# Query and key parts in a scratch buffer: which copies are stored, and which are made by the loads

## The chip, the cores and the metric

The kernel runs on one core of one Trainium2 chip. The metric is device time in microseconds (us); lower is better. Three runs of the kernel before gave 1540.12, 1537.32 and 1542.91 us; their median is 1540.12 us.

## The reference, cut to what matters

The program is three residual blocks over x of shape (8, 512, 128), eight batches of 512 tokens:

```python
x = x + 0.5 * ffn(layernorm(x))     # attention with 16 heads of 8, then a mixture of 8 experts
x = x + attn(layernorm(x))          # 16 query heads of 8, 4 key/value heads, rotary positions
x = x + 0.5 * ffn(layernorm(x))     # the first block again, same weights
# each attention: softmax(q @ k.T / sqrt(8)) @ v, then a projection
```

Each block has one attention over 512 x 512 scores for each of 16 heads and 8 batches, so there are 24 batch attentions in all. The expert part takes, for each token, the expert with the largest gate logit.

## The kernel before, in words

**Tiling.** A batch has 16 heads. Four heads make a *group* (G = 4 groups a batch, J = 4 heads in a group), so there are 24 x 4 = 96 groups. The function `stream` is built twice: with `label` 0 it handles the 8 batches (32 groups) of the first block, with `label` 1 the 16 batches (64 groups) of the second and third. The tokens' expert work is cut into blocks (`experts`), which stand between the steps of the end of one stream and of the opening of the next.

**Split of q and k.** Scores are made by TensorE in float32r. To keep precision, q and k are each split into a high part `hi` and a low part `lo` (the rest), and a score is the contraction over stacked rows: per head 8 rows of each of four products hi*hi, hi*lo, lo*hi, lo*lo. In a tile of 64 partitions, the first 32 rows (`ROWS` = 4 x 8) of `c.Q` hold q parts and those of `c.K` hold k parts. Before, Q has the parts in the order hi, hi, lo, lo and K in the order hi, lo, hi, lo. Behind them come two rows of Q in which `rows_of_max` writes the high and low parts of the row maxima, against rows of -1 in K, so that the transposed scores come out with the maximum already subtracted. The rest of Q's 64 rows of a tile is zero.

**How parts get there.** For batch b, ScalarE copies the projected q and k out of PSUM (`copy_qk`, L1084 and L1086; rotated ones by `high_part`), and `lo` is made by a subtraction: on GpSimd (`low_part`, L719) for batches 1 and later, on VectorE (`low_first`) for batch 0. `hi` and `lo` lie as [128 partitions, 512] (i = 0 is q, i = 1 is k). They go to HBM scratch, `c.q_scratch` and `c.k_scratch`, by `store` (L456), one DMA of 256 KB for each stored part. For batch 0 of a stream ScalarE's queue stores the high parts and SyncE's queue the low ones, with the semaphores `first_stored`; for all others GpSimd's queue does both, with the semaphores `stored`. Before, q_scratch has 32 rows a tile, with each part twice, so q takes four stores a batch, and k takes two.

**Loads.** For each group n, `load(n)` in the SyncE program brings both tiles (2 x 64 partitions) from scratch into one of five slots of Q and K. It first waits for the scores of the group that had the slot, then for q's stores (`stored(sp, 0, ...)`, only at n = 1 and at the first group of a batch), clears 16 rows of each tile from `zero_rows` (L571; not for n < 5 of label 0), loads Q with two DMAs of 128 KB (L582), waits for k's stores likewise, and loads K with four DMAs of 64 KB (L589): each tile twice from the same 16 rows. Group 0 of a stream doesn't go through scratch: `straight` (L466) copies its parts within SBUF.

**Order of the work.** The order on every engine is fixed when the program is built (`Plan`). In the steady stretch, step (n, kt) of TensorE makes four score tiles for the row maxima of group n + 2 (L844), four transposed score tiles of group n for the exponential (L860), and the weighting by v (L873). VectorE reduces the first kind to maxima (L1239), ScalarE exponentiates the second (L1210). The maxima of group n + 1 are split (L1247, L1249), turned by TensorE (L851), copied to SBUF (L1261), and written into Q by SyncE's queue (`rows_of_max`, L601). On that queue the order in the loop over n is: rows_of_max(n + 1), load(n + 4), then a weight load or two. In the opening of a stream's main part it is load(1), load(2), load(3), rows_of_max(0), rows_of_max(1), load(4). TensorE's main part turns the maxima of group 0, waits for the loads of group 1 (`loaded(1)`), makes the maxima scores of group 1, and begins step (0, 0), whose scores wait for the rows of rows_of_max(0).

Of the kernel before, what the change touches and what calls it, by code (L numbers as in the profile page):

```python
# [19 lines left out]
F32 = mybir.dt.float32  # L20
# [8 lines left out]
H, HD = 16, 8  # L29
QT = S // P  # L30
NT = B * QT
G, J = 4, 4
NG = B * G
# [11 lines left out]
KSLOT = PAIRS * S  # L45
TILE = 64
ROWS = 4 * HD
# [7 lines left out]
SLOTS = 5  # L55
# [20 lines left out]
def wait(eng, sem, value):  # L76

    if isinstance(value, int) and value <= 0:
        return
    eng.wait_ge(sem, value)  # L80
# [33 lines left out]
def sems(ctx, nc, tag, names):  # L114

    handles, fields, values = [], [], []
    for entry in names.split():
        name, _, n = entry.partition(":")
        new = [nc.alloc_semaphore(name=f"{tag}_{name}{i}") for i in range(int(n or 1))]
        handles += new  # L120
        fields.append(name)
        values.append(new if n else new[0])

    def clear():
        nc.clear_and_free_semaphores(handles)
        nc.all_engine_barrier()

    ctx.callback(clear)
    return namedtuple("Sems", fields)(*values)
# [259 lines left out]
def stream(nc, c, ctx, a, label, kinds, past, blocks):  # L389
# [6 lines left out]
    if True:  # L396
        s = sems(ctx, nc, f"s{label}", "filled freed evacuated first max_hi split recip max_rows:5 q_loaded:5 k_loaded:5 "
                 "scores probs pv out_copied links dve_links first_stored:2 var_ready std_ready normed renormed stats:2 moments:2 added combined roped hi lo:2 "
                 "stored:2 k_first choices onehot chosen located scattered:2 tabled table tails:2")
# [42 lines left out]

        def stored(eng, i, b):

            size = (64, 32)[i]
            if b in (1, 2):
                eng.wait_ge(s.first_stored[i], size)
            wait(eng, s.stored[i], size * (b - 1))

        def store(eng, i, b, done, parts):  # L450

            at = b % B * G
            for part in parts:
                for copy in range(2 - i):
                    r = HD * ((2 - i) * part + copy)
                    eng.dma_start((c.q_scratch, c.k_scratch)[i][at:at + G, :, r:r + HD, :].rearrange("g t d n -> (g t) (d n)"),  # L456
                                  (hi, lo)[part](b)[i]).then_inc(done, 16)
                    yield

        def straight(eng, i, part):  # L460

            dst, done = ((c.Q, s.q_loaded[0]), (c.K, s.k_loaded[0] if label else s.k_first))[i]
            for tile in range(2):
                for copy in range(2):
                    r = TILE * tile + HD * (2 * part + copy if i == 0 else 2 * copy + part)
                    eng.dma_start(dst[r:r + HD, 0:KSLOT].bitcast(F32).rearrange("d (a n) -> d a n", a=PAIRS),  # L466
                                  (hi, lo)[part](0)[i][2 * HD * tile:2 * HD * (tile + 1), :]).then_inc(done, 16)
                    yield
# [97 lines left out]
        def sync(sp):  # L566
# [6 lines left out]
            def load(n):  # L573
                if n >= SLOTS:
                    sp.wait_ge(s.scores, QT * J * (n - SLOTS + 1))
                g = n % SLOTS
                if n == 1 or n % G == 0:
                    stored(sp, 0, n // G + 1)
                if n >= SLOTS or label:
                    clear_rows(g)  # L580
                for tile in range(2):
                    sp.dma_start(c.Q[TILE * tile:TILE * tile + ROWS, g * KSLOT:(g + 1) * KSLOT].bitcast(F32),  # L582
                                 c.q_scratch[n % NG, tile, :, :]).then_inc(s.q_loaded[g], 16)
                if n == 1 or n % G == 0:
                    stored(sp, 1, n // G + 1)
                for tile in range(2):
                    for copy in range(2):
                        r = TILE * tile + 2 * HD * copy
                        sp.dma_start(c.K[r:r + 2 * HD, g * KSLOT:(g + 1) * KSLOT].bitcast(F32),  # L589
                                     c.k_scratch[n % NG, tile, :, :]).then_inc(s.k_loaded[g], 16)  # L590

            def rows_of_max(n):

# [235 lines left out]
        def tensor(pe):  # L829
# [154 lines left out]
                        project(kind, i)  # L984

            def loaded(n):
                pe.wait_ge(s.q_loaded[n % SLOTS], 32 * (1 + label) + 96 * (n % SLOTS == 0) + 64 * (n // SLOTS))
                if n % SLOTS or label:
                    pe.wait_ge(s.k_loaded[n % SLOTS], 64 * (n // SLOTS + 1) + 64 * (n % SLOTS == 0))
                else:  # L990
                    pe.wait_ge(s.k_first, 128)
                    wait(pe, s.k_loaded[0], 64 * (n // SLOTS))
# [729 lines left out]
def build(nc, a, out):  # L1722
    with ExitStack() as ctx:
# [3 lines left out]
        c = Core()  # L1727
# [36 lines left out]
        c.blocks, c.thresh, c.down = sb("blocks", [P, NBLK]), sb("thresh", [P, HT_ROWS]), sb("down", [P, E])  # L1764
        c.banks = banks = ctx.enter_context(nc.psum_tensor("banks", [P, 8 * 512], F32))
        c.bank = [banks[:, i * 512:(i + 1) * 512] for i in range(8)]
        c.q_scratch = nc.dram_tensor("q_scratch", [NG, 2, ROWS, KSLOT], F32).ap()
        c.k_scratch = nc.dram_tensor("k_scratch", [NG, 2, 2 * HD, KSLOT], F32).ap()
        c.zero_rows = nc.dram_tensor("zero_rows", [2 * HD, KSLOT], F32).ap()
        c.sorted_x = nc.dram_tensor("sorted_x", [HALVES * (E + 1) * REGION, W], F32).ap()  # L1770
# [96 lines left out]
```

## Time and profile before

| | |
|---|---|
| median of three runs | 1540.12 us |
| the profiled execution's own time | 1544.99 us |
| its span, first to last instruction | 1543.3 us |
| granted TensorE clock, mean | 0.965 |
| TensorE / VectorE / ScalarE / GpSimd busy | 90% / 76% / 71% / 42% |
| moved by DMA | 137.57 MB, mean 89 GB/s |
| read from HBM / written to HBM | 79.05 / 53.51 MB |

The profile is one execution. Its own time holds 1.7 us beside the span. Busy shares are means over stages that have different limits: from about 60 to 445 us and from about 620 to 1400 us the two streams run in their steady stretch; between and behind them stands the expert work. Two stretches matter for what the change touches: the opening of the first stream (20 to 60 us) and that of the second (580 to 615 us), in which the first loads from scratch are made.

### The profile page before, as it was taken

To read this page: it belongs to the slowest core of one execution; us is meant where nothing else is said; L and a number is where in the kernel's file an instruction comes from. 1 tells how busy PE (TensorE), PEld (TensorE's weight loads), DVE (VectorE), ACT (ScalarE), POOL (GpSimd) and SP (SyncE) were. 2 spreads that over 40 slices of the span, in tenths; PEclk is the share of its full clock that TensorE was granted. 3 is DMA by queue.
4 is the path that set the end of the run, shared out by engine and by line. 5 is a ranking of instruction groups with operands and counts; after the bars stand their busy time and mean duration, and the time that the engine had idled before them with its cause. 6 is when DMAs were issued, how large, how long until landed. Compare 5 with 4: busy or idle time off the path is not lost.

```text
span 1543.3 us, 34954 instructions
## 1 busy us (share of the span) xinstructions
PE 1388.1 (90%) x12036; PEld 678.6 (44%) x12036; DVE 1177.7 (76%) x1898; ACT 1102.0 (71%) x2124; POOL 644.8 (42%) x983
## 2 busy tenths in 40 slices
PE   3699999999999886999999999999999999999975
PEld 1233334344339874333333333333333343335875
DVE  6788888888955255888888888888888888883541
ACT  2387877787775452788888888887878877777543
POOL 5222344542226555434554353133234544223743
PEclk8699999999999987999999999999999999999998
DMA  5344433432112315423332333333333333201234
GB/s 130 96 134 121 107 102 108 113 95 83 44 29 64 105 52 150 108 67 95 99 84 74 96 95 95 94 81 82 86 92 88 83 91 102 65 23 42 75 95 119
DMA packets 101485, 137.57 MB, mean 89 GB/s; under 512 B 29792, under 2 KB 72160, under 8 KB 101312
## 3 DMA queue, kind: packets, MB, share of 16 engines
q1 hardware_dynamic: 70768, 85.69, 19.6%
q0 software_dynamic: 24256, 45.31, 12.0%
q10 hardware_dynamic: 6288, 4.34, 1.0%
q8 instruction: 100, 1.64, 0.4%
q14 instruction: 73, 0.60, 0.1%
HBM read 79.05 MB, written 53.51 MB: 86 GB/s over the span
## 4 chain that ended last, share of the span: by engine, by line
PE 55%; DVE 27%; issue 7%; DMA 5%; POOL 2%; SPq 2%; ACT 1%; DVEq 0%; POOLq 0%; ACTq 0%
DVE maxima L1239 23%; PE banks L873 15%; PE banks L860 11%; PE banks L844 11%; PE banks L1589 4%; PE banks L901 4%; PE banks L1598 3%; PE banks L927 2%; PE banks L883 2%; DMA k_scratch<-hi 1%; PE banks L908 1%; DVE stats L1317 1%; PE banks L943 1%; DVE split L1247 1%; POOL by_token L1572 1%
## 5 line engine op out<-in xcount | busy, mean ns | idle before, releaser
L1239 DVE TENSOR_REDUCE maxima<-banks 128x2 f32<-128x1024 f32 x768 | 924.5, 1222 | 166.0 <-PE banks L844 157.1
L1210 ACT ACTIVATE work<-banks 128x512 f32<-128x512 f32 x1536 | 829.4, 598 | 169.9 <-PE banks L860 155.1
L844 PE MATMUL banks<-K,Q 64*128 64x512 f32 x1536 | 570.9, 461 | 52.0 <-DVE maxima L1239 34.9
L860 PE MATMUL banks<-Q,K 64*128 64x512 f32 x1536 | 569.7, 453 | 0.4
L873 PE MATMUL banks<-work,V 128*18 128x256 f32 x6144 | 483.4, 387 | 1.5 <-ACT work L1210 0.8
L844 PEld LDWEIGHTS banks<-K,Q 64*128 64x128 f32 x1536 | 229.6, 190 | 206.5 <-DVE maxima L1239 131.8
L860 PEld LDWEIGHTS banks<-Q,K 64*128 64x128 f32 x1536 | 230.5, 187 | 178.2 <-ACT work L1210 133.1
L873 PEld LDWEIGHTS banks<-work,V 128*18 128x18 f32 x6144 | 103.6, 96 | 276.6 <-issue 203.0
L719 POOL TENSOR_TENSOR lo<-full,hi 128x512 fp32r<-128x512 f32 x40 | 51.1, 1276 | 251.2 <-ACT hi L1086 148.0
L1652 DVE COPY work<-w 128x512 f32 x88 | 43.9, 500 | 89.5 <-PE banks L1589 78.0
L1598 PE MATMUL banks<-w,work 128*128 x736 | 102.1, 284 | 2.9 <-issue 1.4
L1572 POOL DMA_INDIRECT by_token<-work x76 | 75.7, 996 | 68.6 <-ACT work L1632 58.9
L1589 PE MATMUL banks<-work 128*128 128x128 f32 x704 | 96.9, 283 | 1.5 <-DVE work L1652 1.5
L1598 PEld LDWEIGHTS banks<-w,work 128*128 128x128 f32 x736 | 93.3, 199 | 4.1 <-issue 3.6
L1589 PEld LDWEIGHTS banks<-work 128*128 128x128 f32 x704 | 89.2, 199 | 4.6 <-issue 2.4
L139 POOL TENSOR_SCALAR root<-moments 128x4 f32<-128x4 f32 x38 | 9.1, 240 | 165.6 <-DVE moments L1324 164.9
L1627 ACT ACTIVATE work<-banks 128x512 f32<-128x512 f32 x92 | 54.8, 596 | 31.8 <-PE banks L1589 31.5
L700 POOL DMA_INDIRECT sorted_x<-N,pos x64 | 65.4, 1022 | 19.9 <-issue 11.9
L1622 ACT ACTIVATE work<-banks,ln 128x128 f32<-128x128 f32 x92 | 41.8, 455 | 35.3 <-PE banks L1582 28.1
L545 POOL TENSOR_TENSOR full<-full,cos_sb 128x512 f32<-128x512 f32 x12 | 15.4, 1285 | 116.6 <-ACT swap L1080 116.5
L140 POOL TENSOR_TENSOR rstd<-root,minus_half 128x4 f32<-128x4 f32 x52 | 54.1, 1040 | 4.4
L1084 ACT ACTIVATE full<-banks 128x512 f32<-128x512 f32 x44 | 26.3, 597 | 40.5 <-PE banks L901 34.8
(193 smaller groups left out, 1269.8 us busy)
## 6 DMA issues: line engine op xcount, KB each, us to landing
Q<-q_scratch SPq DMA_DIRECT2D x188, 128.0 KB, 2.6
K<-k_scratch SPq DMA_DIRECT2D x376, 64.0 KB, 2.5
Q<-zero_rows SPq DMA_DIRECT2D x182, 64.0 KB, 2.2
q_scratch<-hi POOLq DMA_DIRECT2D x40, 256.0 KB, 4.7
q_scratch<-lo POOLq DMA_DIRECT2D x40, 256.0 KB, 6.8
k_scratch<-hi POOLq DMA_DIRECT2D x20, 256.0 KB, 4.5
k_scratch<-lo POOLq DMA_DIRECT2D x20, 256.0 KB, 6.1
work<-sorted_x SPq DMA_DIRECT2D x76, 66.0 KB, 1.9
```

What stands on the lines that cost most here:

```text
L140: link(eng.tensor_tensor(out, half, c.minus_half[:, :], ALU.pow))
L700: nc.gpsimd.indirect_dma_start(c.sorted_x[:, :], bass.IndirectOffsetOnAxis(ap=c.pos[:, t:t + 1], axis=0), c.rows[:, t, :], None).then_inc( ...
L844: fill(nc.tensor.matmul(bank, q4[parts(j), n % SLOTS, j // 2, qt * P:(qt + 1) * P], k4[parts(j), n % SLOTS, j // 2, :], start=True, stop=T ...
L860: nc.tensor.matmul(scp[x % EXPS][:, :], k4[parts(j), n % SLOTS, j // 2, kt * P:(kt + 1) * P], q4[parts(j), n % SLOTS, j // 2, :], start=Tr ...
L873: ins = nc.tensor.matmul(outp[32 * j:32 * j + 2 * V1, q], v4[:, n // G % VSLOTS, kt, n % G // 2, j, V1 * odd:V1 * odd + 2 * V1], prob[:, k ...
L901: fill(nc.tensor.matmul(bank, w[:, i * D:(i + 1) * D], c.zT[:, :], start=True, stop=True), kind, b)
L1210: nc.scalar.activation(prob[:, kt, j ^ 1, :], scp[x % EXPS][:, :], ACT.Exp, scale=SCALE).then_inc(s.probs, 1)
L1239: nc.vector.tensor_reduce(c.maxima[:, at:at + 9:8], c.banks[:, k * S:(k + 2) * S].rearrange("p (m n) -> p m n", m=2), AX.X, ALU.max).then_ ...
L1572: nc.gpsimd.indirect_dma_start(c.by_token[:, :], bass.IndirectOffsetOnAxis(ap=x_sb(i)[:, D:D + 1].bitcast(U32), axis=0), y_sb[i % ring], N ...
L1589: ins = nc.tensor.matmul(hp[i % 2][:, t * P:(t + 1) * P], w1(i)[:, t * P:(t + 1) * P], uT[i % 2], start=True, stop=True)
L1598: ins = nc.tensor.matmul(yp, h[i % 2][:, t * P:(t + 1) * P], cols(c.w2, at + t * D, D), start=(t == 0), stop=(t == HT - 1))
L1627: nc.scalar.activation(h[i % 2], hp[i % 2][:, :], ACT.Gelu_apprx_tanh).then_inc(s.gelu, 1)
```

## The change

q's parts are stored once instead of twice, so q_scratch has 16 rows a tile like k_scratch. The order of the parts in the tiles is exchanged: Q now holds hi, lo, hi, lo and K holds hi, hi, lo, lo, which gives the same four products. Q is loaded by four DMAs of 64 KB for a group, each tile twice from its 16 rows. K is still loaded by four DMAs of 64 KB, but each of them reads the 8 rows of one part and writes them to 16 partitions, by a source pattern of 2 x 8 rows whose outer step is zero. Counts of semaphores follow. The copies in `straight` keep number and size, and change their rows.

```diff
         def stored(eng, i, b):
-            size = (64, 32)[i]
+            size = 32
             if b in (1, 2):
                 eng.wait_ge(s.first_stored[i], size)
             wait(eng, s.stored[i], size * (b - 1))
@@ store
             for part in parts:
-                for copy in range(2 - i):
-                    r = HD * ((2 - i) * part + copy)
-                    eng.dma_start((c.q_scratch, c.k_scratch)[i][at:at + G, :, r:r + HD, :].rearrange("g t d n -> (g t) (d n)"),
-                                  (hi, lo)[part](b)[i]).then_inc(done, 16)
-                    yield
+                r = HD * part
+                eng.dma_start((c.q_scratch, c.k_scratch)[i][at:at + G, :, r:r + HD, :].rearrange("g t d n -> (g t) (d n)"),
+                              (hi, lo)[part](b)[i]).then_inc(done, 16)
+                yield
@@ straight
-                    r = TILE * tile + HD * (2 * part + copy if i == 0 else 2 * copy + part)
+                    r = TILE * tile + HD * (2 * copy + part if i == 0 else 2 * part + copy)
@@ load(n)
                 for tile in range(2):
-                    sp.dma_start(c.Q[TILE * tile:TILE * tile + ROWS, g * KSLOT:(g + 1) * KSLOT].bitcast(F32),
-                                 c.q_scratch[n % NG, tile, :, :]).then_inc(s.q_loaded[g], 16)
+                    for copy in range(2):
+                        r = TILE * tile + 2 * HD * copy
+                        sp.dma_start(c.Q[r:r + 2 * HD, g * KSLOT:(g + 1) * KSLOT].bitcast(F32),
+                                     c.q_scratch[n % NG, tile, :, :]).then_inc(s.q_loaded[g], 16)
                 if n == 1 or n % G == 0:
                     stored(sp, 1, n // G + 1)
                 for tile in range(2):
-                    for copy in range(2):
-                        r = TILE * tile + 2 * HD * copy
+                    for part in range(2):
+                        r = TILE * tile + 2 * HD * part
                         sp.dma_start(c.K[r:r + 2 * HD, g * KSLOT:(g + 1) * KSLOT].bitcast(F32),
-                                     c.k_scratch[n % NG, tile, :, :]).then_inc(s.k_loaded[g], 16)
+                                     c.k_scratch[n % NG, tile, HD * part:HD * (part + 1), :].rearrange("(o d) n -> o d n", o=1)
+                                     .broadcast_to((2, HD, KSLOT))).then_inc(s.k_loaded[g], 16)
@@ loaded(n)
-                pe.wait_ge(s.q_loaded[n % SLOTS], 32 * (1 + label) + 96 * (n % SLOTS == 0) + 64 * (n // SLOTS))
+                pe.wait_ge(s.q_loaded[n % SLOTS], 64 + 32 * label + 64 * (n % SLOTS == 0) + 96 * (n // SLOTS))
@@ build
-        c.q_scratch = nc.dram_tensor("q_scratch", [NG, 2, ROWS, KSLOT], F32).ap()
+        c.q_scratch = nc.dram_tensor("q_scratch", [NG, 2, 2 * HD, KSLOT], F32).ap()
```

In the second stream's opening, one step fewer stands in ScalarE's generator of first stores (six instead of seven), so that ScalarE issues k's high store and `high_part(1, 1)` one expert block earlier.

## Rows read from the trace of the kernel before

**Rows 1.** Timeline of SyncE's queue, steady stretch: start us, duration us, queue, line, what.
```profile
100.88 1.28 SPq L601 DMA_DIRECT2D Q<-maxT  x2
...
113.23 1.27 SPq L601 DMA_DIRECT2D Q<-maxT  x2
```

**Rows 2.** Waits of TensorE, whole span: us in total, times, longest.
```profile
PE banks L844 <- DVE maxima L1239: 34.9, 90, 1.0
...
PE banks L844 <- DMA K<-k_scratch: 5.0, 1, 5.0
...
PE banks L844 <- DMA Q<-maxT: 0.7, 1, 0.7
```

**Rows 3.** Waits of SyncE's queue, whole span, same columns.
```profile
SPq L601 <- DVE maxT L1261: 624.2, 94, 11.2
...
SPq L571 <- DMA q_scratch<-lo: 12.3, 1, 12.3
SPq L447 <- DMA q_scratch<-lo: 10.3, 1, 10.3
```

**Rows 4.** Timeline of the first opening: start, duration, engine, line, idle before.
```profile
44.28 0.40 PE L851 MATMUL banks<-ident,split 128*32 128x128 f32 x1 [2.93 <-DVE split L1249]
...
45.42 1.69 SPq L589 DMA_DIRECT2D K<-k_scratch  x4
...
49.05 1.22 PE L844 MATMUL banks<-K,Q 64*128 64x512 f32 x4 [4.37 <-issue]
...
52.71 1.35 SPq L601 DMA_DIRECT2D Q<-maxT  x2
...
58.12 1.19 PE L860 MATMUL banks<-Q,K 64*128 64x512 f32 x2
```

**Rows 5.** Timeline of the second opening, same columns.
```profile
597.30 1.29 SPq L571 DMA_DIRECT2D Q<-zero_rows  x2
...
598.90 0.32 PE L851 MATMUL banks<-ident,split 128*32 128x128 f32 x1 [3.86 <-DVE split L1249]
...
600.46 1.69 SPq L589 DMA_DIRECT2D K<-k_scratch  x4
...
604.25 1.22 PE L844 MATMUL banks<-K,Q 64*128 64x512 f32 x4 [5.03 <-DMA K<-k_scratch]
...
609.60 8.91 SPq L601 DMA_DIRECT2D Q<-maxT  x4
...
613.31 1.19 PE L860 MATMUL banks<-Q,K 64*128 64x512 f32 x2
```

**Rows 6.** Stretches: busy us by engine, PE clock, DMA share of 16 engines, GB/s.
```profile
12.00:14.00 2.00, 1.09 (x4) 0.71 (x4) 1.82 (x10) 0.02 (x1) 0.00 (x0) 1.00 1.06 299
28.00:30.00 2.00, 0.00 (x0) 0.00 (x0) 0.00 (x0) 0.08 (x1) 1.70 (x3) 0.74 0.45 141
...
28.00:46.00 18.00, 6.39 (x17) 2.34 (x17) 10.90 (x19) 0.08 (x1) 9.26 (x15) 0.53 0.67 172
580.00:600.00 20.00, 12.47 (x92) 9.82 (x91) 11.10 (x19) 7.51 (x17) 17.10 (x19) 0.97 0.73 194
...
852.50:853.00 0.50, 0.50 (x8) 0.30 (x4) 0.48 (x3) 0.50 (x2) 0.00 (x0) 1.00 0.77 287
...
1000.00:1100.00 100.00, 94.83 (x862) 37.57 (x860) 87.05 (x121) 80.65 (x153) 30.24 (x52) 1.00 0.33 87
```

**Rows 7.** DMA issues: queue, count, KB each, median us from issue to landing.
```profile
K<-k_scratch SPq DMA_DIRECT2D x376, 64.0 KB, 2.5
...
q_scratch<-hi POOLq DMA_DIRECT2D x40, 256.0 KB, 4.7
...
w<-in_w SPq DMA_DIRECT2D x16, 256.0 KB, 2.8
```

**Rows 8.** The tile maxT: duration of the issue, ns min/median/max.
```profile
L601 SPq DMA_DIRECT2D Q<-maxT x192: 596/616/2256, 52.7 to 1393.3; - x192
```

**Rows 9.** The chain of waits near 1129 us: start, us, what.
```profile
1128.84 8.22 DMA Q<-maxT
```

## The prediction

> **What bounds the kernel now.** I read the busy shares first (the page's, in the table above): TensorE 90% of the span, VectorE 76%. In the steady stretch TensorE has more: 94.83 us of 100, at the full clock, while the DMA engines are 33% busy [rows 6]; a group takes 12.4 us there, from one issue of the rows of maxima to the next [rows 1]. So there TensorE sets the time, with VectorE's reduction of maxima close beside it. Next come TensorE's own waits. The costliest in sum is for VectorE, 34.9 us in 90 pieces. The DMA waits are single events: 5.0 us once for K from scratch, 0.7 us once for the rows of maxima [rows 2]. The waits of SyncE's queue say where the stores hurt: 10.3 and 12.3 us, once each, for q's low store, in the openings of the two streams. In all later groups it waits 624.2 us in 94 pieces for VectorE's copy of the maxima, 6.6 us of idle time a group: the queue is early there [rows 3].
>
> So the change can pay in two places, and I followed both by the timeline. First opening: k's stores have landed at 45.42, when K's loads go out (q's some 3 us before); TensorE had turned the maxima of group 0 at 44.28 to 44.68 and begins group 1 at 49.05; the first score of step (0, 0) is at 58.12, after the rows of group 0's maxima were issued at 52.71 [rows 4]. Second opening: q's at 597.30, k's at 600.46, maxima turned by 599.22, group 1 at 604.25, rows issued at 609.60, first score at 613.31 [rows 5].
>
> **The change, part by part.**
>
> *Stores.* q loses two of four stores of 256 KB a batch, k keeps two. In each opening two batches are stored (0 and 1), so four DMAs of 0.262 MB go, 1.05 MB of 3.15. From 28 to 46 us the engines move 172 GB/s, from 580 to 600 us 194 GB/s [rows 6], so the same backlog drains 6.1 and 5.4 us sooner. In the second opening ScalarE also issues k's high store one expert block sooner; I allow 1.6 us for it, an estimate, and take 7.0 there. K's loads can then go out at 45.4 - 6.1 = 39.3 and 600.4 - 7.0 = 593.4. Bounds: nothing, if the landing waits for GpSimd's stores that remain; 9 and 10 us, if the whole of the batch's share (4 of 6 stores) scales it. In the steady stretch GpSimd issues two DMAs fewer a batch; it is 42% busy, and nothing is gained.
>
> *Q's loads.* Two DMAs of 128 KB become four of 64 KB: the same bytes, two issues more. An issue takes 0.42 us (1.69 us for four with K's) [rows 4]. 0.9 us a group on SyncE's queue, against 6.6 us of idle time: nothing. In the openings three loads stand ahead of the rows of group 0's maxima, 2.5 us; it matters in a rival below.
>
> *K's loads.* Count and size stay, the pattern doesn't: the source is now 2 x 8 rows, the destination 16 partitions. No K load of before looks like that. I ask how many of the 16 DMA engines such a DMA uses. From 28 to 30 us little but stores and straight copies are in flight, with a backlog, and the engines' share is 0.45, against 1.06 for the loads of x at 12 us [rows 6]. Those stores have a leading count of 8 on the HBM side, against 128 partitions: half of the engines fits a spread over 8. A store of that form needs 4.7 us to land, a weight load of the same 256 KB, 128 against 128, 2.8 us [rows 7]. The one DMA with a leading 2 against 16 is that of the maxima (2 partitions of Q from 16 of maxT); its issue takes 616 ns instead of 420 [rows 8]. I therefore take the new K load to run on 2 engines. Bounds: on 16, nothing changes; on 2, all K traffic goes over one pair.
>
> The Trainium skill ("DMA: Bandwidth & Descriptors", section "Why a DMA increments its semaphore by 16 and not by 1") says the same as a rule: the number of engines is the largest up to 16 that divides the slowest non-unit dimension of both patterns, and on this kind of queue they are the lowest-numbered ones. It gives 2 for this load, always the same pair; the half share above agrees with its 8 for the stores. With that page's 27 GiB/s an engine a group's K loads would take 4.5 us rather than the 5.6 us below, and the sum would fall by about 7 us.
>
> *Price of the pair.* From 852.5 to 853 us the engines move 287 GB/s at a share of 0.77 [rows 6]: 287 / (0.77 x 16) = 23.3 GB/s an engine. A group's K loads are 4 x 65.5 KB = 262 KB: 262 / 46.6 = 5.6 us on a pair, where 16 engines need 0.7 us. The slow end is the stretch at 12 us, 299 / (1.06 x 16) = 17.6 GB/s: 7.4 us. In the steady stretch the pair has 5.6 us of K and at most its share of the rest, 0.33 x 12.4 = 4.1 us, in a group of about 12.4 us: 9.7 us, it fits. The rows of maxima, which go over the same queue, are issued before the next group's loads, after the last ones have drained, and they tolerate much: once they took 8.22 us [rows 9] and TensorE waited 0.7 us [rows 2]. So about 7.5 us are free, and loads have two groups of lead. Nothing is lost there; I give back the 0.7 us, since half of q's stores that collided are gone.
>
> In the openings it is not hidden: the rows of maxima of group 0 stand behind three groups of K. First opening: K's first issue at 39.3, 2.3 us for latency (2.5 to land [rows 7] less its data), 3 x 5.6 = 16.8, two groups of Q at 0.7 each: 1.4. They land at 59.8, and the first score starts then, not at 58.12: +1.7 us. Group 1 itself would land at 39.3 + 2.3 + 5.6 + 0.7 = 47.9, earlier than today's 49.05. Second opening: 593.4 + 2.3 + 16.8 + 1.4 + 0.7 for two groups of cleared rows = 614.6 against 613.31: +1.3 us. SyncE's issues don't bind more: at 0.62 us for each K load and 0.42 for each of Q, three groups take 13 to 16 us. So what the stores give, 6.1 and 7.0 us, is used up by the pair.
>
> *Sum.* +1.7 + 1.3 - 0.7 = +2.3 us. The profiled execution's own time is 1544.99 us, span 1543.3 and 1.7 around it; the sum against it is 1547.3. The median of the runs, 1540.12, lies 4.9 us lower, and the forecast with it: 1542.4, so **1542 us**, in effect no change.
>
> **Rivals.**
>
> *K stays wide (16 engines).* Then TensorE's readiness is the bound. First opening: group 1 at 44.7 instead of 49.05, -4.4 us. Second: 599.2 instead of 604.25, -5.0, less 0.5 for SyncE, whose 18 issues for three groups become 24 (597.30 to 609.60 was 12.3 us, 14.8 from 590.3 on, rows at 605.1 + 3.7 = 608.8 against 608.3). Straight copies with less beside them may give 0.7, the steady stall 0.7: -10.3, **1530 us**. For it: count and bytes are the same, and each run of data is still a row of 4 KB. Against: the half share and the issue time above.
>
> *The pair is slow (the other side).* Place: the two engines that carry all K loads. At 17.6 GB/s K takes 7.4 us a group, 1.8 more; three groups in each opening, 5.4 us twice, 10.8 us. In the first stream, with weights loaded beside it, the pair would be at 7.4 + 4.1 to 5 of 12.4 us, and the rows of maxima become late by some tenths in a few groups: 2 more. +15 us, **1555 us**. It decides from about 20.8 GB/s downward: 6.3 us a group, 0.7 more six times, +4.2 on +2.3, over the bound of no change. For it: 16 engines together showed that rate under load. Against: two engines share HBM and SBUF with less, and the 23.3 was itself measured at 77% share.
>
> *The stores don't drain sooner.* If q's and k's first stores still landed at 42 and 45 us (and 597 and 600), because they wait for what GpSimd has queued, the K traffic comes on top: 2.3 + 6.1 + 7.0 = +15 us, **1556 us**. For it: the low store took 12 us to land though SyncE had issued it early. Against: GpSimd's own stores are halved for q too.
>
> **How the numbers follow.** Forecast 0.62, K wide 0.19, slow pair 0.13, no sooner draining 0.06. Under the forecast each opening is good to about 4 us, so its own range is 1534 to 1549: faster by over 0.3% (4.6 us, about what a measurement of this kernel can tell) 0.15, within 0.62, slower 0.23. K wide: 0.9 faster, 0.1 same. The others are slower. Faster 0.62 x 0.15 + 0.19 x 0.9 = 0.26; same 0.62 x 0.62 + 0.02 = 0.41; slower 0.14 + 0.13 + 0.06 = 0.33. The range takes in K wide and most of the slow pair: 1529 to 1554 us.
>
> **What would show it.** Right: q's and k's stores waited for until about 36 and 39 us, and 590 and 593; issues of K's loads at 0.6 us instead of 0.42, with no landing time told; TensorE's first scores at 58 to 61 and 613 to 616 us behind "DMA Q<-maxT"; group 1 begun sooner than 49.05; the steady stretch unchanged at 12.4 us a group and 95 of 100 us busy. Wrong: K's issues at 0.42 us and landing at 2.5 us (K wide); waits for Q<-maxT all along the stream (slow pair, or a pair at its limit); SyncE's waits for first stores ending where they did; or a change of the steady rate, for which I have no mechanism.

## The result, and the profile after

The changed kernel takes 1544.59 us (median of 20 runs, 1541.54 to 1548.13) beside 1540.6 us for the kernel before on the same chip (20 runs): ratio 1.0024 [1.0013, 1.0034]. In a second comparison of the two it was 1.0029 [1.0012, 1.0046]. That is 4 us more: a small loss, whose interval lies above 1 both times. (One of the 12 runs of the changed kernel in the second comparison took 3968 us and is left out of its ratio.) The forecast was 1542 in the range 1529 to 1554. The profiled execution has an own time of 1543.83 us and a span of 1542.1, 1.2 us *under* the profiled one of before; the last part of the section on the prediction comes back to that.

The first view is that of SyncE's waits in the whole span: us in total, times, longest.

```profile
SPq L603 <- DVE maxT L1263: 534.4, 93, 12.6
...
SPq L570 <- DMA q_scratch<-lo: 4.8, 1, 4.8
...
SPq L447 <- DMA q_scratch<-lo: 4.1, 1, 4.1
```

Against [rows 3] the two waits for q's low store have gone from 10.3 and 12.3 us to 4.1 and 4.8. The waits of TensorE, same columns:

```profile
PE banks L846 <- DVE maxima L1241: 33.6, 86, 1.0
...
PE banks L846 <- DMA Q<-maxT: 8.9, 3, 4.7
...
PE banks L846 <- DMA K<-k_scratch: 3.1, 1, 3.1
```

Against [rows 2], the wait for the rows of maxima has grown from one of 0.7 us to 8.9 us, nearly all of it in two waits, one an opening. The timeline of SyncE's queue in the first opening (start, duration, what):

```profile
32.60 6.17 SPq L583 DMA_DIRECT2D Q<-q_scratch  x4
38.81 2.57 SPq L590 DMA_DIRECT2D K<-k_scratch  x4
...
47.66 2.49 SPq L590 DMA_DIRECT2D K<-k_scratch  x4
50.20 14.95 SPq L603 DMA_DIRECT2D Q<-maxT  x4
```

and TensorE's in the same time, which begins with the maxima of group 0:

```profile
30.06 1.22 PE L846 MATMUL banks<-K,Q 64*128 64x512 f32 x4 [5.08 <-DMA Q<-lo]
...
42.02 0.40 PE L853 MATMUL banks<-ident,split 128*32 128x128 f32 x1 [2.93 <-DVE split L1251]
47.27 1.22 PE L846 MATMUL banks<-K,Q 64*128 64x512 f32 x4 [4.85 <-issue]
...
59.92 0.79 PE L846 MATMUL banks<-K,Q 64*128 64x512 f32 x1 [4.01 <-DMA Q<-maxT]
59.92 1.22 PE L862 MATMUL banks<-Q,K 64*128 64x512 f32 x2
```

K's first load goes out at 38.81 instead of 45.42, group 1 begins at 47.27 instead of 49.05, and yet the first score (line 862) comes at 59.92 instead of 58.12 [rows 4], after 4.01 us in which TensorE had nothing but the rows of maxima to wait for. The rows were issued at 50.20 (the 14.95 us of that line take in the rows of group 1, issued later). The second opening, SyncE's queue and then TensorE:

```profile
589.81 2.94 SPq L590 DMA_DIRECT2D K<-k_scratch  x4
...
603.57 15.19 SPq L603 DMA_DIRECT2D Q<-maxT  x4
```

```profile
596.74 0.37 PE L853 MATMUL banks<-ident,split 128*32 128x128 f32 x1 [3.76 <-DVE split L1251]
600.22 1.22 PE L846 MATMUL banks<-K,Q 64*128 64x512 f32 x4 [3.11 <-DMA K<-k_scratch]
613.54 0.79 PE L846 MATMUL banks<-K,Q 64*128 64x512 f32 x1 [4.68 <-DMA Q<-maxT]
```

The same picture beside [rows 5]: K's load 10.7 us earlier (589.81 against 600.46), group 1 4.0 us earlier, the first score 0.2 us later. The form of the K load, by its instructions of the first stream (ns, min/median/max):

```profile
L590 SPq DMA_DIRECT2D K<-k_scratch x112: 575/592/638, 67.3 to 408.2; - x112
```

and its line in the page's DMA issues (KB each, us from issue to landing):

```profile
Q<-q_scratch SPq DMA_DIRECT2D x376, 64.0 KB, 2.3
K<-k_scratch SPq DMA_DIRECT2D x376, 64.0 KB
```

An issue of before took 420 ns and had a landing time, 2.5 us [rows 7]; this one takes 592 and has none. (A missing landing time alone tells little: the 8 by 2 pattern of a later run has none either.)

The engines' share shows how many of them carry these loads. Stretches with nothing in flight but K's loads and the rows of maxima behind them, one in each opening (busy us of PE, PEld, DVE, ACT, POOL; clock; DMA share; GB/s):

```profile
49.00:59.00 10.00, 4.77 (x12) 1.73 (x12) 8.67 (x10) 0.00 (x0) 1.53 (x4) 0.50 0.13 52
606.00:612.00 6.00, 2.19 (x6) 0.66 (x6) 4.62 (x6) 0.00 (x0) 0.00 (x0) 0.50 0.13 52
```

A share of 0.13 of 16 engines is 2.1 engines. The last K load was issued by 50.15, so several loads were waiting together, and still no more than two engines worked: they all use the same pair. It moves 52 GB/s, 26 an engine, so a group's 262 KB take 5.0 us on it, an estimate from this rate. At last the stretches of [rows 6] (same columns):

```profile
28.00:46.00 18.00, 6.38 (x17) 2.33 (x17) 10.91 (x19) 0.00 (x0) 10.03 (x17) 0.54 0.53 136
...
1000.00:1100.00 100.00, 94.89 (x860) 37.61 (x860) 87.04 (x117) 80.45 (x153) 27.90 (x48) 1.00 0.27 77
```

Beside [rows 6] the DMA share while the stores drain is 0.53 instead of 0.67, and 0.27 instead of 0.33 in the steady stretch, where TensorE is as busy as it was (94.89 of 100 us against 94.83).

### The profile page after: what moved, and what is told of

It is laid out like the page before. It is cut to its first block and busy times, and to the rows that moved or that the text cites. A ratio compares the mean times of both kernels' runs of the same rounds, so it can differ in the third digit from the quotient of the medians.

```text
span 1542.1 us, 35094 instructions
## 1 busy us (share of the span) xinstructions
PE 1384.1 (90%) x12036; PEld 675.3 (44%) x12036; DVE 1178.2 (76%) x1898; ACT 1101.5 (71%) x2124; POOL 618.1 (40%) x939
## 5 line engine op out<-in xcount | busy, mean ns | idle before, releaser
L1654 DVE COPY work<-w 128x512 f32 x88 | 44.1, 502 | 86.6 <-PE banks L1591 74.2
L1629 ACT ACTIVATE work<-banks 128x512 f32<-128x512 f32 x92 | 54.8, 596 | 30.4 <-PE banks L1591 29.9
L1624 ACT ACTIVATE work<-banks,ln 128x128 f32<-128x128 f32 x92 | 41.8, 455 | 32.6 <-PE banks L1584 24.4
L1086 ACT ACTIVATE full<-banks 128x512 f32<-128x512 f32 x44 | 26.3, 597 | 41.1 <-PE banks L903 35.4
```

The source lines that it names most:

```text
L1629: nc.scalar.activation(h[i % 2], hp[i % 2][:, :], ACT.Gelu_apprx_tanh).then_inc(s.gelu, 1)
```

## The experiments

The theory: two effects of nearly the same size cancel. q's stores halved make K's loads go out sooner; the new pattern of K's loads puts them on a pair of DMA engines, and the rows of group 0's maxima queue behind three groups of them. The rival after the result was that neither does much. The runs were made in three groups, the first on a chip where the kernel before took 1550.72 us (22 runs), the others where it took 1540.38 and 1540.82 (29 and 11 runs). So only ratios are compared between groups, and a ratio is good to about 0.2%, 3 us. The first group is the four runs up to the repeat on the inside; the second goes from "the two kernels again" to "the pair beside spread stores"; the third is the rest.

Four runs leave out something so as to change one thing: in both "K wide" and in "the pair alone" K and Q hold the parts in orders in which two of the four products are missing or doubled, and in "the pair beside spread stores" the copies of K stand one behind the other where they should alternate. Their scores are wrong. Counts, bytes and the order of work are the same; which expert a token gets may differ, but their times between the streams (134.5 to 140.3 us in the later groups) don't stand out from the others'.

**K wide, first time.** From the changed kernel, K's load takes back the pattern of before, 16 rows on 16; K's rows come in the wrong order.

```diff
-  c.k_scratch[n % NG, tile, HD * part:HD * (part + 1), :].rearrange("(o d) n -> o d n", o=1)
-  .broadcast_to((2, HD, KSLOT))).then_inc(...)
+  c.k_scratch[n % NG, tile, :, :]).then_inc(...)
```

> The changed kernel, but each K load reads the 16 rows of both parts as one block, as before the change, so K holds hi, lo, hi, lo against Q's hi, lo, hi, lo: two of the four products are missing or doubled, everything else (counts, bytes, order) is that of the changed kernel. Theory (the K loads run on a pair of the 16 DMA engines, and the rows of maxima of group 0 wait behind three groups of them): K's issues back at 0.42 us and landing in about 2.5; group 1 begun as soon as TensorE has turned the maxima (42.4 and 597.1 us), first scores at about 51.5 and 606.5 instead of 59.9 and 613.5; about 15 us less than the changed kernel, 1529 us, ratio to before 0.993. Rival (SyncE's queue: four issues more a group and slower ones, not the engines): only 12 x 0.17 = 2 us less in each opening, about 1540 us. Rival (the loss is in the steady stretch): a change there, the openings as in the changed kernel.

Measured: 0.9962 [0.9945, 0.9978]. Without the pair the saved stores are a gain, 6 us. It is less than expected, since the stores themselves still land late: group 1 began 1.7 and 3.0 us after TensorE had turned the maxima of group 0 (42.4 to 44.1, 601.6 to 604.6). Neither rival fits: the queue's would have left 1540 us, a ratio of 1.000, and the steady stretch is as in the others.

**q stored twice again.** The second half of the stores is put back, into a scratch that nobody reads; the loads stay as changed.

```diff
-            size = 32
+            size = (64, 32)[i]
...
+                for to in ((c.q_scratch, c.q_spare), (c.k_scratch,))[i]:
```

> The changed kernel with the removed stores put back: each part of q is stored a second time, into a scratch buffer that nobody reads, and the waits count them. Theory (the stores removed let the first loads go out 6 to 10 us sooner, and that alone covers the pair's price): loads of K at about 45 and 597 us again, first scores 6 to 8 us later in each opening, 13 us more than the changed kernel, 1557 us, ratio to before 1.011. Rival (the bytes stored do not matter, the landing waits for something else): as the changed kernel, 1544.

Measured: 1.0117 [1.0099, 1.0135], about 0.9% or 14 us over the changed kernel's 1.0024 and 1.0029. K's first load went out at 44.09 in the first opening, instead of 38.81 and 33.89 in the two profiles of the changed kernel. In the second it went out at 612.15, but everything on this chip is later by then; counted from TensorE's first maxima of the second stream it is 10.9 us instead of 6.2 and 7.0. With the pair present the first score follows K's first load, so the whole of this is seen in the time.

**Rows of maxima first.** They are sent after the first group's loads instead of after the third's.

```diff
-                for n in range(1, 4):
-                    load(n)
+                load(1)
                 rows_of_max(0)
+                for n in range(2, 4):
+                    load(n)
```

> The changed kernel with one line moved: the rows of maxima of group 0 are sent after load(1), ahead of load(2) and load(3). Theory: they then stand behind one group of K on the pair, and land before TensorE has finished group 1's maxima: first scores at about 56 and 609.5 instead of 59.9 and 613.5, waits for DMA Q<-maxT in the openings gone, 8 us less than the changed kernel, 1536 us, ratio 0.997. Rival (the first scores wait for the loads of group 2, or SyncE's wait for VectorE's copy delays those): no gain, 1544, with a wait for K<-k_scratch at step (0, 0).

Measured: 0.9991 [0.9975, 1.0006], some 5 us under the changed kernel's 1.0024 to 1.0029, which were measured in other groups; 8 were expected. The waits for the rows are gone from the first scores. What is late next is K itself; TensorE's timeline in the second opening of this kernel:

```profile
601.00 0.37 PE L854 MATMUL banks<-ident,split 128*32 128x128 f32 x1 [3.82 <-issue]
607.38 1.22 PE L847 MATMUL banks<-K,Q 64*128 64x512 f32 x4 [6.00 <-DMA K<-k_scratch]
616.44 1.19 PE L863 MATMUL banks<-Q,K 64*128 64x512 f32 x2
```

It waits 6.00 us for K and then no longer for the rows: from the turn to the first score 15.4 us, where the changed kernel needs 16.8. The stall moved, and a part of it was saved.

**The repeat on the inside.** K's source is written as 8 rows by 2 copies, not 2 by 8, and q's scratch has its two parts in alternating rows, so that its store has (g t d), 64 rows, in front. The straight copies and Q's loads change their rows with it. So two things change at once; "the pair beside spread stores" below separates them.

```diff
-  c.k_scratch[...].rearrange("(o d) n -> o d n", o=1).broadcast_to((2, HD, KSLOT))
+  c.k_scratch[...].rearrange("d (o n) -> d o n", o=1).broadcast_to((HD, 2, KSLOT))
...
-  c.q_scratch[at:at + G, :, r:r + HD, :].rearrange("g t d n -> (g t) (d n)")
+  c.q_scratch[at:at + G, :, :, part, :].rearrange("g t d n -> (g t) d n")
```

> A full version with the same saving of stores, in which the rows of the parts alternate inside 16 rows: the K loads' source is 8 rows x 2 copies (leading count 8 instead of 2), q's scratch has 64 leading rows for its stores (was 8), Q's loads stay 16 rows on 16. Theory (the number of engines follows the smaller leading count): K's issues stay near 0.6 us, but a group of K takes 1.4 us on 8 engines instead of 5.6; first scores at about 51.5 to 53 and 606.5 to 608, 13 to 15 us less than the changed kernel, 1529 to 1531 us, ratio 0.993. Rival (the broadcast pattern itself is slow, on however many engines): as the changed kernel, 1544.

Measured: 0.9936 [0.9920, 0.9952]. TensorE's waits for the rows of maxima are 1.2 us in sum, against 8.9, and group 1 begins 0.3 us after the turn in both openings (40.3 to 40.6, 593.3 to 593.6). The rival, that the repeated pattern is slow on any number of engines, is out.

**The two kernels again.** Both unchanged, for a second profile of each and one more comparison.

> The kernel before, unchanged, for a trace of it from the same chip as the others of this call: ratio 1.000 within 0.002. If the expert work between the streams is what differs from chip to chip, its stretch from the last group of stream one to the first maxima of stream two differs from the 137.7 us of the first profile, and the steady stretches (374 and 773 us) don't.

> The changed kernel, unchanged, on the same chip: ratio 1.002 to 1.004. Theory: from the turn of group 0's maxima to the first score 17 to 18 us in the first opening and about 16.8 in the second (13.8 and 14.4 before), K's first load issued 6 and 8 to 10 us sooner than before, steady stretches within 0.5 us of before. Rival (steady stretch, or the expert stretch pays): a difference there of 3 us or more that repeats the first pair's sign.

Measured: 0.9997 [0.9981, 1.0013] and 1.0029 [1.0012, 1.0046]. The second profile of the changed kernel shows how far one opening differs between executions of one program. The loss repeats, but the openings aren't as they were expected: from the turn to the first score it takes 14.2 and 16.3 us (expected 17 to 18 and 16.8), and K's first load goes out 11.1 and 5.7 us sooner than in the second profile of before (expected 6, and 8 to 10). Between the streams the changed kernel took 1.0 and 1.9 us longer than the kernel before in the two pairs (138.7 against 137.7, 140.7 against 138.8), under the 3 us of the rival. SyncE's queue:

```profile
31.26 2.59 SPq L583 DMA_DIRECT2D Q<-q_scratch  x4
33.89 2.57 SPq L590 DMA_DIRECT2D K<-k_scratch  x4
```

K's first load goes out 4.9 us sooner than in the first profile (33.89 against 38.81) and TensorE has its first score at 56.00, 3.9 us sooner.

**All of it.** The alternating rows for k's scratch too, and the rows of maxima after the first group's loads.

```diff
-  (c.q_scratch, c.k_scratch)[i][at:at + G, :, r:r + HD, :].rearrange("g t d n -> (g t) (d n)")
+  (c.q_scratch, c.k_scratch)[i][at:at + G, :, :, part, :].rearrange("g t d n -> (g t) d n")
...
+                load(1)
                 rows_of_max(0)
+                for n in range(2, 4):
```

> The version with alternating rows of parts, and beside it k's scratch alike (64 leading rows for k's stores too) and the rows of maxima of group 0 sent after load(1). Theory: everything lands before TensorE is ready, so both openings are as short as its own work: 9.4 us from turn to first score in the first, 9.0 to 9.4 in the second (10.2 with the eight-engine version), so 1 us less than that version, ratio to before 0.992 to 0.993. Rival (the order matters less, and load(2) is now late since SyncE waits for VectorE's copy): 1 to 2 us more, 0.994 or above.

Measured: 0.9889 [0.9864, 0.9914], less than the 0.992 expected; the run with k's stores alone, below, looks for the reason.

**The pair beside spread stores.** "The repeat on the inside" with K's pattern put back to 2 by 8 (K's rows in another order).

```diff
-  c.k_scratch[...].rearrange("d (o n) -> d o n", o=1).broadcast_to((HD, 2, KSLOT))
+  c.k_scratch[...].rearrange("(o d) n -> o d n", o=1).broadcast_to((2, HD, KSLOT))
```

> The eight-engine version with the K loads' source pattern turned back to 2 x 8 rows, so they run on a pair again; q's stores keep their 64 leading rows. The rows that K gets are not those that belong there (the copies stand one behind the other instead of alternating); counts and bytes are those of the changed kernel. Theory: K's loads go out as early as in the eight-engine version (about 31.5 and 585.4 us), and the pair's price stays: first scores 20 to 21 us after K's first issue, at 52 and 607 instead of 49.7 and 603.5; 5 to 6 us more than the eight-engine version, ratio 0.997. Rival (what the eight-engine version gains over the changed kernel is the spread of K alone): as the changed kernel, 1.002.

Measured: 0.9957 [0.9942, 0.9972]. TensorE waits for the rows of maxima again:

```profile
PE banks L847 <- DMA Q<-maxT: 9.0, 3, 5.4
```

Beside 0.9936 and (below) 0.9910 for the same kernel with 8 by 2, the order of two dimensions of one access pattern is worth 3 to 7 us here. The openings alone would say about 10 (the table below). And beside the changed kernel's 1.0024 and 1.0029, with the same pattern for K, q's stores with 64 rows in front are worth some 10 us.

**The pair alone.** From the kernel before: only K's load has the new pattern; all stores and q's loads are as they were (K's rows in the wrong order).

```diff
-                    for copy in range(2):
-                        r = TILE * tile + 2 * HD * copy
+                    for part in range(2):
+                        r = TILE * tile + 2 * HD * part
...
-  c.k_scratch[n % NG, tile, :, :]).then_inc(...)
+  c.k_scratch[n % NG, tile, HD * part:HD * (part + 1), :].rearrange("(o d) n -> o d n", o=1)
+  .broadcast_to((2, HD, KSLOT))).then_inc(...)
```

> The kernel before with one edit: its K loads take the changed kernel's source pattern of 2 x 8 rows (K then holds hi, hi, lo, lo against Q's hi, hi, lo, lo, so two of the four products are missing or doubled). q is stored twice and loaded by two DMAs as before. Theory (the pair's price is independent of the stores and falls on the rows of maxima in both openings): K's issues 0.6 us, first scores 20 to 23 us after K's first issue instead of 12.7, which is 8 us later in each opening; 12 to 16 us more than before, about 1554 us, ratio 1.008 to 1.010. From the two runs in hand (before to the K-wide version 0.996, that to the changed kernel 1.0065) at least 1.006. Rival (the pair costs only where loads start early): within 0.003 of before.

Measured: 1.0098 [1.0081, 1.0115], 15 us. TensorE's waits for DMAs in this kernel, the longest:

```profile
PE banks L845 <- DMA K<-k_scratch: 7.9, 1, 7.9
PE banks L845 <- DMA Q<-lo: 7.7, 1, 7.7
PE banks L845 <- DMA Q<-maxT: 6.6, 2, 3.8
```

The wait for K in the second opening is 7.9 us (5.0 in [rows 2]), and the first scores wait again for the rows of maxima. The 7.7 for Q<-lo belongs to the kernel before as well: 7.5 in its second profile. The engines' share behind the last K load is as in the changed kernel:

```profile
53.00:63.00 10.00, 5.51 (x16) 1.74 (x13) 9.49 (x10) 0.00 (x0) 1.09 (x2) 0.50 0.13 52
```

**K wide, second time.** The same kernel as the first, in the third group.

> The K-wide version once more, on whatever chip comes: Theory: ratio to before 0.996 again (0.994 to 0.998), that is stores halved are worth 6 us, first scores 10.7 and 12 us after the turn. Rival (the chip of the first time hid a gain, its expert stretch was 147 us): 0.993 or less.

Measured: 0.9943 [0.9927, 0.9960], as expected. Here group 1 begins 0.3 us after the turn in both openings. While K's and Q's loads are in flight, the engines' share is four times the pair's:

```profile
44.00:47.00 3.00, 2.27 (x6) 0.86 (x6) 3.00 (x3) 0.00 (x0) 2.60 (x6) 0.50 0.55 152
```

The pages count the packets of SyncE's queue (packets, MB, share of 16 engines), first in the changed kernel, then in this one, then with 8 by 2 ("the repeat on the inside", second time):

```profile
q1 hardware_dynamic: 68240, 85.15, 18.9%
q1 hardware_dynamic: 73504, 85.17, 20.2%
q1 hardware_dynamic: 70512, 85.16, 20.0%
```

For the same bytes, K wide has 5264 packets more than 2 by 8, which is 14 for each of the 376 K loads, and 8 by 2 has 2272 more, 6 for each load and 16 over. If each engine that takes part adds one packet of its own to a load, which is an inference, this fits 16, 8 and 2 engines. Between the kernel before and the pair alone the difference is 5264 again (70768 against 65504).

**The repeat on the inside, second time.**

> The eight-engine version once more, beside the next one. 0.992 to 0.995.

Measured: 0.9910 [0.9894, 0.9925], just below the 0.992 to 0.995 expected. In the same group K wide has 0.9943, and in the first group the two had 0.9936 and 0.9962: 4 and 5 us less with q's stores 64 rows in front, and no pair in either.

**k's stores spread, nothing moved.** "All of it" without the moved rows of maxima.

> The eight-engine version with k's scratch in alternating rows too, so k's stores have 64 leading rows, and the rows of maxima left where they were. If k's stores are what made the last version better than this one (0.989 against 0.994): 0.989 to 0.991, with K's first loads in the second opening at about 577 instead of 585 us. If the moved line did it: 0.993 to 0.995, and then the second opening has a wait for Q<-maxT of about 1 us.

Measured: 0.9888 [0.9872, 0.9904], 1522.73 us, 17 us under the kernel before and the best of all. With 0.9889 for "all of it" the moved line adds nothing that can be seen once K is no longer on a pair. What k's stores add to "the repeat on the inside" is about 3 us in the same group (0.9910), where the two intervals overlap, so this part is likely and not shown. The page's DMA issues of this kernel:

```profile
q_scratch<-hi POOLq DMA_DIRECT2D x20, 256.0 KB, 2.5
q_scratch<-lo POOLq DMA_DIRECT2D x20, 256.0 KB, 2.7
```

A store of 256 KB with 64 rows in front lands in 2.5 us, with 8 in 4.2 in the changed kernel and 4.7 before [rows 7]. In the second opening of this kernel (SyncE, then TensorE) K's first load goes out at 577.05 and TensorE waits 0.79 us at the first score. The 577 that was expected as a sign of k's stores is none: "the repeat on the inside" on the same chip has 577.85, and the 585 of its first profile belonged to the other chip.

```profile
577.05 3.17 SPq L589 DMA_DIRECT2D K<-k_scratch  x4
```

```profile
584.69 0.37 PE L852 MATMUL banks<-ident,split 128*32 128x128 f32 x1 [3.38 <-DVE split L1250]
...
594.44 0.79 PE L845 MATMUL banks<-K,Q 64*128 64x512 f32 x1 [0.79 <-DMA Q<-maxT]
```

**All runs in one table.** "Opening 1" is the time of the first score, "opening 2" the time from TensorE's first maxima of the second stream to its first score, both read from each timeline, one profile each, in us. The difference of their sum is against 85.8, the mean of the two profiles of before. The last column is the measured ratio less 1, times 1540.

| kernel | opening 1 | opening 2 | sum | difference | measured |
|---|---|---|---|---|---|
| before, two profiles | 58.1, 57.7 | 29.0, 26.8 | 87.1, 84.6 | 0 | 0 |
| changed, two profiles | 59.9, 56.0 | 29.9, 29.6 | 89.8, 85.6 | +4.0, -0.2 | +3.7, +4.5 |
| pair alone | 64.0 | 35.4 | 99.4 | +13.6 | +15.1 |
| q stored twice again | 64.9 | 34.6 | 99.5 | +13.7 | +18.0 |
| K wide, twice | 53.2, 50.9 | 25.5, 24.1 | 78.7, 75.0 | -7.1, -10.8 | -5.9, -8.8 |
| rows of maxima first | 55.6 | 28.4 | 84.0 | -1.8 | -1.4 |
| pair, stores spread | 54.3 | 30.3 | 84.6 | -1.2 | -6.6 |
| repeat on the inside, twice | 49.7, 50.5 | 24.6, 24.6 | 74.3, 75.1 | -11.5, -10.7 | -9.9, -13.9 |
| all of it | 48.5 | 22.8 | 71.3 | -14.5 | -17.1 |
| k's stores spread | 48.8 | 22.2 | 71.0 | -14.8 | -17.2 |

The measured order is nearly that of the openings. The two columns differ by 5.4 us at most and by no more than 3.2 in nine of twelve pairs; two profiles of one kernel differ by up to 4.2 us in this sum. That is the support for saying that most of the effect lies in the openings.

## Why the prediction was right

**The steady stretch** stayed as it was, as forecast: 94.89 of 100 us busy, and in every kernel the time from the second group's first score to the last group's is 372.4 to 375.4 us in the first stream and 771.1 to 775.2 in the second. The pair alone has 374.1 and 771.1, the two profiles of before 374.0 and 773.1, 372.6 and 771.9. Neither saved stores nor K on a pair is seen there. The pair held its load.

**The stores** freed K's loads at 38.81 and 589.81, forecast 39.3 and 593.4. The first figure is partly luck: the second profile has 33.89, and in the first SyncE spent 6.17 us on four issues of Q's loads, which I had put at 1.7. The waits for q's first stores ended at 32.6 and 587.0 and not at 36 and 590; so the stores drained sooner than a backlog in proportion to the bytes gives, and the issues of Q's loads took part of it back. Over both openings K's first loads went out 17.3 us sooner in the first pair of profiles and 16.8 in the second, where 13.1 were forecast; how it divides differs (6.6 and 10.7, then 11.1 and 5.7). The rival in which they don't drain sooner is out: its sign, waits that end where they did, is absent.

**Q's loads** were priced at nothing. That holds in the steady stretch. In the first opening their issue was on the path in one of the two profiles, with 4.5 us more than priced.

**K on a pair.** The issue time changed from 420 to 592 ns with no landing told, as forecast. That the loads run on two engines is seen in the share of 0.13. The step's size can be read from four openings: from K's first issue to the first score it took 21.1 and 23.7 us in the first profile and 22.1 and 22.6 in the second (33.89 to 56.00, 589.76 to 612.38); forecast were 20.5 and 21.2. With the forecast's own 2.3 for latency, 1.4 for Q and 0.7 for cleared rows taken off, three groups of K took 17.4, 19.3, 18.4 and 18.2 us, so 5.8 to 6.4 a group where 5.6 was forecast. But the pair itself is faster than that: at its 52 GB/s a group takes 5.0 us, between the 5.6 and the 4.5 of the prediction. So the rate was put a little too low, and 2.3 to 4.2 us an opening went to something the sum had no term for. Stores and Q's loads that still shared the engines are likely (the share is 0.53 from 28 to 46 us), but no run separates it. That the term stands in the time with its full price is shown by the pair alone, +15.1 us; the forecast contained 16 (what it let the stores give, 13.1, and 3.0 over it). That the stores give what was said is shown by putting them back, +14 (forecast 13.1). Both together came out at +4, forecast +2.3. So by these runs two large terms of opposite sign were each right within 1 or 2 us, with intervals of 3 to 4 us on each. By the profiles both were put too small: the stores gave 17 us, not 13.1, and the way from K's first load to the first score grew by 19.3 and 17.9 us (from 12.7 and 12.9, 12.8 and 14.0), not 16. These two errors took each other back. The mechanism was right; that the sum came out within 2 us of the measured loss is partly luck.

What is shown is that 2 by 8 keeps two engines busy, and that the order 2 by 8 against 8 by 2 of the same bytes changes the wait for the rows (8.9 and 9.0 us against 1.2 and 1.1) and the time, with stores spread, by 3 to 7 us. While K's and Q's loads of "the repeat on the inside" are in flight, the share is 0.41, 6.6 engines:

```profile
39.00:41.00 2.00, 0.00 (x0) 0.00 (x0) 1.93 (x11) 0.00 (x0) 0.16 (x1) 0.50 0.41 119
```

Which two of the 16 the pair is, no view tells. This is as the rule of the Trainium skill has it ("DMA: Bandwidth & Descriptors", section "Why a DMA increments its semaphore by 16 and not by 1"), by which the slowest dimension that isn't 1, on both sides, sets how many engines take part; the 2.1 engines here agree with its 2. It also gives a direction for repair, and the runs with 8 rows for K and 64 for the stores followed it.

**K wide as a rival** was priced at -10.3 us, 1530. The kernel made for it came out at -5.9 and -8.8. The mechanism was right. The first run falls short of the price since the stores still landed 1.7 and 3.0 us after TensorE was ready, where the rival had taken TensorE's readiness for the bound; in the second run they landed in time, and its interval (-6 to -11 us) takes in the price. One reading in this rival was off: the 12.3 us of SyncE's queue, 597.30 to 609.60, hold 24 issues and not 18, as each group has two that clear rows, so they become 30; the 6 more are the same. And the chance of "same" adds up to 0.40, not 0.41.

**What I had left out:** the straight copies of group 0 land sooner with fewer stores beside them. TensorE begins the first maxima at 30.06 and 29.85 in the two profiles of after, at 32.3 and 33.4 in those of before, and at 32.97 with the stores put back, and so turns them at 42.02 instead of 44.28. The prediction had 0.7 us for this in one rival only. It gave the changed kernel nothing, because the rows of maxima came later than that anyway; but in the kernels where the pair is gone it is 2 to 6 us of the gain (first maxima at 27.43 with k's stores spread).

**What the profiles leave open.** The profiled executions of the two kernels differ by -1.2 us in one pair (1542.1 against 1543.3) and by +5.5 in the other (1543.5 against 1538.0), around the measured +4. A part of the first can be read. At the first score the changed kernel is 1.8 us behind, at the second group's first score 0.2 ahead (72.4 against 72.6), because the granted clock came back to full sooner. Stretches of before:

```profile
66.00:67.00 1.00, 1.00 (x8) 0.40 (x4) 0.70 (x1) 0.10 (x2) 0.00 (x0) 0.75 0.70 156
...
102.00:103.00 1.00, 1.00 (x10) 0.17 (x6) 0.95 (x1) 0.73 (x2) 0.92 (x2) 0.50 0.06 15
```

and of after:

```profile
66.00:67.00 1.00, 1.00 (x16) 0.43 (x12) 1.00 (x1) 0.83 (x3) 0.00 (x0) 1.00 0.31 95
...
102.00:103.00 1.00, 1.00 (x14) 0.21 (x12) 0.97 (x2) 0.96 (x3) 0.98 (x1) 1.00 0.12 47
```

At 66 us before still has half the clock (1.2 of 2.4 GHz) for part of the microsecond, after has the full one; and before is at half once more at 102 us, which after isn't. In the second pair it is the other way round at 657 us (0.50 in after, 1.00 in before). The forecast had no term for it, and one profile each can't tell how often which kernel is hit. The rest lies in the expert stretch between the streams and in the tail, which the change doesn't touch: from the last group of the first stream to the first maxima of the second the kernels took 134.4 to 140.7 us where the kernel before takes 1540, and 141.1 to 147.7 in the first group. Of the former the four profiles with spread stores are the shortest (134.4 to 137.2 against 137.7 to 140.7), and so is the one of the latter (141.1 against 143.7 to 147.7). Part of their gain beyond the openings may come from this stretch; why was not tried.

## What to carry to other kernels

When an edit changes the shape of a DMA, look at its leading count on both sides before its bytes: the same 64 KB as 2 by 8 cost 15 us in two openings, and the engines' share in a stretch where only this DMA is in flight (0.13 of 16 here) tells how many carry it. In turn, 8 by 2 and scratch rows ordered so that the stores lead with 64 gave a kernel 17 us faster than the one before. A narrow DMA is free while its queue is early (all 376 K loads here but the 24 of the two openings), and is paid where something small and urgent is sent behind several of them; look at the beginnings of streams. And a sum near nothing may be two terms near 15 us: test each alone, as the small sum can't tell them from two nothings.

## What the runs showed that was not expected

SyncE's issue of a DMA isn't a fixed 0.42 us while stores drain: four issues of Q's loads took 6.17 us in one execution, 2.59 in another of the same kernel, and 1.8 when nothing was behind. The issue time isn't a measure of how many engines take part either: with 8 by 2 an issue of K takes 644 to 657 ns, longer than the 592 of 2 by 8, in the faster kernel. And a store of q, 256 KB, that leads with 64 rows lands in 2.5 to 3.3 us where the one with 8 takes 4.2 to 5.3 in the changed kernel (k's: 3.0 and 3.7 in "all of it" against 4.5 and 5.6).
